# Expert tiles that add their gated results to the output rows, with the addition in the middle of the next tile, and expert weights split over two tiles

## The reference, cut to what matters

```python
N, C, E, H = 4096, 256, 8, 1024
x = x + graph_attention(layernorm(x), adj, Wq, Wk, Wv)     # adj is sparse: a few neighbours a row
xn = layernorm(x)
probs = softmax(xn @ W_router)
topk_p, topk_i = top_k(probs, 2)
topk_p = topk_p / topk_p.sum(-1)
combine = sum of one_hot(topk_i) * topk_p                  # [N, E], two entries a token
for e in range(E):
    h = relu(xn @ W1[e] + b1[e])
    y = h @ W2[e] + b2[e]
    out = out + combine[:, e:e+1] * y
x = x + out
```

## Time and profile before

| | |
|---|---|
| median of 3 runs | 1069.51 us (1068.68 to 1070.36) |
| the profiled execution | 1069.15 us, its span 1067.5 us |
| PE busy | 799.0 us (75%) |
| PEld busy | 731.2 us (68%) |
| DVE busy | 673.1 us (63%) |
| ACT busy | 465.5 us (44%) |
| POOL busy | 440.1 us (41%) |
| mean granted TensorE clock over the span | 0.855 |

### The profile page before, as it was taken

One profiled execution on the slowest core, in us unless ns is written; L12 is line 12 of the kernel. 1 busy time (PEld: TensorE's weight loads), 2 busy tenths in 40 slices (PEclk: granted clock), 3 DMA queues, 4 the chain that ended last, 5 costly groups with the idle time before them and its releaser, 6 DMA issues.

```text
span 1067.5 us, 23696 instructions
## 1 busy us (share of the span) xinstructions
PE 799.0 (75%) x6721; PEld 731.2 (68%) x6722; DVE 673.1 (63%) x1972; ACT 465.5 (44%) x1309; POOL 440.1 (41%) x440
## 2 busy tenths in 40 slices
PE   2559987997799862254606999999999999999900
PEld 1458876886788751253606988889888898889800
DVE  9867877777688653486275465565565646554555
ACT  2333544343355531143303665655555566565600
POOL 5277777777777732167771000000000000007465
PEclk8578999998899985655557999999999999999955
DMA  9741431422321110222356324241423332124345
GB/s 267 242 109 28 105 103 31 108 71 59 81 51 25 28 31 1 72 86 99 138 182 207 118 74 128 81 141 64 138 79 118 100 116 69 59 79 141 105 144 181
DMA packets 108904, 108.32 MB, mean 101 GB/s; under 512 B 18275, under 2 KB 98100, under 8 KB 108720
## 3 DMA queue, kind: packets, MB, share of 16 engines
q1 hardware_dynamic: 85680, 65.32, 20.1%
q0 software_dynamic: 23168, 42.22, 13.4%
HBM read 93.10 MB, written 40.37 MB: 125 GB/s over the span
## 4 chain that ended last, share of the span: by engine, by line
PE 45%; issue 19%; DVE 15%; POOL 13%; DMA 5%; ACT 2%; DVEq 1%; POOLq 1%; SPq 0%; ACTq 0%
PE psE L1179 10%; POOL nbr L439 7%; PE psH L1168 6%; PE psH L1169 6%; PE psH L1170 6%; PE psE L1181 5%; PE psY L1017 4%; POOL expert_in L486 4%; PE codes L980 2%; DMA xg<-expert_out,gpos 2%; DVE prod L593 2%; PE psQ L1027 1%; PE psX L1155 1%; PE psL L1131 1%; DVE best L575 1%
## 5 line engine op out<-in xcount | busy, mean ns | idle before, releaser
L439 POOL DMA_INDIRECT nbr<-xn_rows,idx x256 | 263.1, 1028 | 108.9 <-issue 104.9
L898 DVE TENSOR_TENSOR h_lo<-z_all,h_hi 128x256 fp32r<-128x256 f32 x296 | 125.2, 423 | 156.4 <-ACT h_hi L1354 156.4
L1353 ACT ACTIVATE z_all<-psH,b1e 128x256 f32<-128x256 f32 x296 | 142.0, 480 | 173.4 <-PE psH L1170 173.4
L1179 PE MATMUL psE<-w_parts,h_hi 128*128 128x512 f32 x552 | 210.2, 407 | 1.7 <-DVE h_lo L898 1.4
L1168 PE MATMUL psH<-x_hi,w_hi 128*128 128x256 f32 (+1 forms) x592 | 167.0, 282 | 13.0 <-issue 6.8
L575 DVE MAX8 best<-codes 128x8 f16<-128x1024 f32 x128 | 150.4, 1222 | 36.4 <-PE codes L980 34.0
L1169 PE MATMUL psH<-x_lo,w_hi 128*128 128x256 f32 (+1 forms) x592 | 167.4, 283 | 0.0
L1170 PE MATMUL psH<-x_hi,w_lo 128*128 128x256 f32 (+1 forms) x592 | 167.0, 282 | 0.0
L1181 PE MATMUL psE<-w_parts,h_lo 128*128 128x256 f32 x552 | 155.4, 281 | 0.0
L1354 ACT ACTIVATE h_hi<-psH,b1e 128x256 fp32r<-128x256 f32 x296 | 141.1, 477 | 0.0
L1017 PEld LDWEIGHTS psY<-diag,nbr 128*128 128x128 f32 x1024 | 133.5, 210 | 7.2 <-issue 4.7
(11 more groups left out here) (258 smaller groups left out, 1096.5 us busy)
## 6 DMA issues: line engine op xcount, KB each, us to landing
adj_in<-in_adj SPq DMA_DIRECT2D x8, 2048.0 KB, 11.1
w_raw<-in_L_ffn_W POOLq DMA_DIRECT2D x16, 1024.0 KB, 5.8
x_in<-expert_in SPq DMA_DIRECT2D x38, 256.0 KB, 2.7
expert_out<-y_out SPq DMA_DIRECT2D x37, 256.0 KB
early_out<-y_out SPq DMA_DIRECT2D x32, 256.0 KB, 2.5
nbr<-xn_rows,idx POOLq DMA_INDIRECT x264, 2.2
x_all<-in_x SPq DMA_DIRECT2D x4, 1024.0 KB, 9.2
xn_rows<-row_all SPq DMA_DIRECT2D x4, 1024.0 KB, 5.0
```

The source lines that it names most:

```text
L439: pool.indirect_dma_start(nbr[:, u, k, :], None, xn_rows, bass.IndirectOffsetOnAxis(ap=idx[:, u, k:k + 1], axis=0), bounds_check=N - 1, oo ...
L898: dve.tensor_tensor(h_lo[:, hc, :], h_f[:, hc, :], h_hi[:, hc, :].bitcast(F32), ALU.subtract).then_inc(hl_ready, 1)
L1179: pe.matmul(psE[:, q, :], h_hi[:, hc, m], w2_parts[:, b, hc].rearrange("p s c -> p (s c)"), start=(hc == 0), stop=False)
L1353: act.activation(h_f[:, hc, :], psH[:, hc % 4, 0:T], ACT.Relu, bias=b1e[:, b, hc:hc + 1])
```

## The change

- `expert_in`'s rows get four more columns (`CX` = C + 4): the token's number (`TOK`), its first expert plus E (`FIRST`), and the difference of its two top logits (`LESS`). VectorE writes them into `xg` (`extras_ready`). Rows that only fill a region up carry the token number N, which the bounds check of the indirect DMAs leaves out.
- x2 is stored to the output (`store_x2`), one quarter after another during routing.
- For each tile GpSimd gathers the tokens' present output rows into `acc`, VectorE computes the gate from the extra columns (`gate_of`, four small operations), adds gate x `y_sum` to `acc` (`add_rows`), and GpSimd scatters the result to the output. `add_rows` and `gate_of` stand in front of chunk 4 of the next tile. At the border between two experts the gather waits until the last scatter has landed.
- The two result tables, their positions and gates, the 64 gathers of result rows, the mixing and the last stores go.
- VectorE splits W1's four pieces in an expert's first tile and W2's four in its second, at chunks 1, 3, 5 and 7.
- SyncE, not GpSimd, loads the raw weights.
- VectorE's and ScalarE's programs of the expert stage are written out for each expert, and ScalarE reads `b1T` directly.

```diff
@@ SyncE
+            def load_weights(e, m):
+                if not isinstance(e, int) or e > 0:
+                    wait_alone(sp, w_split, (e - 1) * SPLITS + (m + 1) * (SPLITS // 2))
+                sp.dma_start(matrices[m][1][:], matrices[m][0][bass.ds(e, 1)].rearrange("a (k p) h -> p (a k) h", p=P)).then_inc(w_raw[m], 16)
...
-            load_tile(0, 0)
-
-            with sp.Fori(total, MAX_TILES + 1) as n:
-                sp.dma_start(rows_of(expert_out, n), zero_rows[:].to_broadcast([P, TS, C])).then_inc(rest_zeroed, 16)
...
-            with sp.Fori(1, early + 1) as n:
-                load_tile(n, tile_row(n))
-                store_tile(n - 1, True)
...
+            def tiles(e, weights):
+                count = sp.value_load(plan[0:1, 0, bass.ds(e, 1)], min_val=1, max_val=N // T)
+                before = sp.value_load(plan[0:1, 1, bass.ds(e, 1)], min_val=0, max_val=MAX_TILES)
+                load_tile(before, e * REGION)
+                with sp.If(count > 1):
+                    load_tile(before + 1, e * REGION + T)
+                if weights:
+                    load_weights(e + 2, 0)
+                    load_weights(e + 2, 1)
+                with sp.If(count > 2):
+                    with sp.Fori(2, count) as i:
+                        load_tile(before + i, e * REGION + i * T)
+            with sp.Fori(0, E - 2) as e:
+                tiles(e, True)
+            with sp.Fori(E - 2, E) as e:
+                tiles(e, False)
@@ GpSimd
-            wait_alone(pool, yo_stored, total * 16 + 16)
-            with pool.Fori(0, NG // 2) as g:
-                fetch(g * 2, 0)
-                fetch(g * 2 + 1, 1)
...
+            def rows_of_tile(n, after):
+                wait_alone(pool, marks_ready, n + 2)
+                pool.tensor_copy(tok_next[:], marks[:, :, 0]).then_inc(tok_taken, 1)
+                wait_alone(pool, tok_taken, n + 2)
+                if after:
+                    wait_alone(pool, y_scattered, n * (TS * 16))
+                for q in range(TS):
+                    pool.indirect_dma_start(acc[:, q, :], None, out, bass.IndirectOffsetOnAxis(ap=tok_next[:, q:q + 1], axis=0),
+                                            bounds_check=N - 1, oob_is_err=False).then_inc(acc_ready, 16)
+
+            def add_tile(done):
+                wait_alone(pool, acc_ready, done * (TS * 16))
+                pool.tensor_copy(tok_now[:], tok_next[:]).then_inc(tok_kept, 1)
+                wait_alone(pool, tok_kept, done)
+                for q in range(TS):
+                    wait_alone(pool, y_ready, done * TS + q + 1)
+                    pool.indirect_dma_start(out, bass.IndirectOffsetOnAxis(ap=tok_now[:, q:q + 1], axis=0), y_out[:, q, :], None,
+                                            bounds_check=N - 1, oob_is_err=False).then_inc(y_scattered, 16)
@@ VectorE
+            def add_rows(done):
+                wait_alone(dve, acc_ready, done * (TS * 16))
+                wait_alone(dve, gate_step, done * 4)
+                wait_alone(dve, y_free, done)
+                for q in range(TS):
+                    wait_alone(dve, yo_ready, done * TS + q + 1)
+                    dve.scalar_tensor_tensor(y_out[:, q, :], y_sum[:, q, :], gate[:, 3, q:q + 1], acc[:, q, :],
+                                             ALU.mult, ALU.add).then_inc(y_ready, 1)
...
+            def tile(n, e, split=None, first=False, alone=None):
                 for hc in range(HC):
...
+                    if hc == HC // 2:
+                        if not first:
+                            add_rows(n)
+                        gate_of(n, e)
+                    splitting = split is not None and hc % 2 == 1
+                    c = (split or 0) * (SPLITS // 2) + hc // 2
+                    if splitting:
+                        next_weights_hi(e, c)
                     dve.wait_ge(hf_ready, n * HC + hc + 1 + 4)
                     dve.tensor_tensor(h_lo[:, hc, :], h_f[:, hc, :], h_hi[:, hc, :].bitcast(F32), ALU.subtract).then_inc(hl_ready, 1)
...
+                    if splitting:
+                        next_weights_lo(e, c)
```

More of the change, by code:

```diff
@@ L359, in _ @@
                 sp.sem_inc(xg_free, 1)
+                store_x2(2 + b)
             sp.wait_ge(norm_ready, NT // QT)
@@ L517, in _ @@
+            rows_of_tile(0, False)
+            with pool.Fori(0, E - 1) as e:
+                tiles(e, True)
+            tiles(E - 1, False)
         @block.vector
@@ L902, in tile @@
+                if alone is not None:
+                    with dve.If(alone):
+                        for c in range(SPLITS // 2, SPLITS):
+                            next_weights_hi(e, c)
+                            next_weights_lo(e, c)
                 rest_of_x(n + 1)
-                wait_alone(dve, yo_stored, n * 16 + 16)
                 for q in range(TS):
@@ new lines, in count_of, with before_of @@
+            def count_of(e):
+                return dve.value_load(plan[0:1, 0, e:e + 1], min_val=1, max_val=N // T)
+            def before_of(e):
+                return dve.value_load(plan[0:1, 1, e:e + 1], min_val=e, max_val=MAX_TILES)
+            rest_of_x(0)
+            count, before = count_of(0), 0
+            for e in range(E):
+                last = e + 1 == E
+                tile(before, e, None if last else 0, e == 0, None if last else count < 2)
+                if not last:
+                    next_count, next_before = count_of(e + 1), before_of(e + 1)
@@ L915, in tiles @@
                 with dve.If(count > 1):
-                    with dve.Fori(1, count) as i:
+                    tile(before + 1, e, None if last else 1)
+                with dve.If(count > 2):
+                    with dve.Fori(2, count) as i:
                         tile(before + i, e)
-            rest_of_x(0)
-            with dve.Fori(0, E // 2 - 1) as e:
-                tiles(e * 2, 1)
-                tiles(e * 2 + 1, 0)
-            tiles(E - 2, 1)
-            tiles(E - 1, None)
-            dve.sem_inc(mixed, GT)
@@ L940, in _ @@
-            dve.wait_ge(lower_fetched, 16 * NT)
-            place(0, 0)
-            first = 0
-            for rows in (z_all[:, NT // 2:NT, :], w1_raw[:].rearrange("p k (j c) -> p (k j) c", c=C), w2_raw[:]):
-                groups = rows.shape[1] // GT
-                with dve.Fori(0, groups // 2) as i:
-                    g = i * 2 + first
-                    place(g + 1, 1)
-                    mix(g, 0, lambda u: row(rows, i * (2 * GT) + u))
-                    if first + groups < NG:
-                        place(g + 2, 0)
-                    mix(g + 1, 1, lambda u: row(rows, i * (2 * GT) + (GT + u)))
-                first += groups
+                if not last:
+                    count, before = next_count, next_before
@@ L955, in _ @@
+            add_rows(before + count)
         @block.tensor
@@ L1359, in attention_and_experts @@
+            count, before = count_of(0), 0
+            for e in range(E):
+                tile_of(before, e)
+                if e + 1 < E:
+                    next_count, next_before = count_of(e + 1), before_of(e + 1)
+                with act.If(count > 1):
+                    with act.Fori(1, count) as i:
+                        tile_of(before + i, e)
+                if e + 1 < E:
+                    count, before = next_count, next_before
     return nc
```

272 lines of the change are left out of this document (110 added, 162 removed).

## The result

The changed kernel takes 1085.93 us (median of 3 runs, 1083.92 to 1085.99) against 1069.51 before: a ratio of 1.0147, interval 1.0124 to 1.017. It is slower, by 16 us; the prediction had forecast 12.5. The profiled execution has a span of 1084.1 us and a mean granted clock of 0.847.

A forecast was written before the change was run, and what follows sets the result against it. TensorE, busy 430.5 of the expert stage's 446.4 us, was taken as the bound, with a separate 53.5 us tail. 1067.5 - 48.2 + 1.9 - 5.6 + 64.8 = 1080.4, with 1.65 outside the span 1082 us; 8-in-10 range 1058 to 1098.

The forecast's parts named there:

- Deciding term, SyncE's queue: Expert's third tile load queued behind W2, which awaits the last split: TensorE waits 8.8 us, six times; bounds 6.9 and 11.
- t0: Time of TensorE's transposes after an expert's second tile, when it wants the third tile; last split predicted 2.1 us later.
- The clock: After each of six waits for the third tile, TensorE restarts at 1.2 GHz: 2.0 us each, bounds 0 and 4.
- The rival in which the clock stays up: Third tile's load overlaps or overtakes W2, clock stays up: 6.35 us per expert, 1055 us; chance 0.18.
- The gap that the prediction named as a sign: Between TensorE's transposes: about 22 us in six second tiles, 11.8 elsewhere.
- Splitting in two tiles: VectorE's weight splits spread over an expert's first two tiles: 0.8 us less for each of seven experts, -5.6.
- Start of the stage: Before the first x_in: two SyncE table loads, +1.6 us, and three small VectorE operations, +0.3; together +1.9.
- The 0.3 for the routing: Three small VectorE operations in front of `placed`, before the expert stage: +0.3 us.
- Tail: After the last tile, gathers, additions and output stores go; two additions, two scatters and a landing remain: 48.2 us removed.
- Additions at no cost: add_rows in mid-tile finds its gathered old rows landed: cost 0; if transfers crowd, up to 1 us a tile, 37 us.
- The rival's mechanism: Gathers and scatters land behind 1 MB loads, VectorE stands in add_rows: 1096 us, or 1119 in all tiles; chance 0.22.
- programs written out per expert: Fetching VectorE's and ScalarE's longer programs may show at branches: 0 to 0.5 us for each of 14, taken as 0.

## Why the prediction was right, point by point

- Deciding term, SyncE's queue. Right in place, cause and number of times: six waits, of 8.55 us against 8.8. That the size is so near is partly luck, since inside it two errors cancel: the last split came 1.2 us after t0 and not 2.1, and the tile was used 7.3 after W2's issue and not 6.4. The tile landed 7.0 us after W2's issue (5.9 after its own), where the trace's own start had given 6.3. The Trainium skill, DMA: Bandwidth & Descriptors, section "Anatomy of one DMA", has its fit for DMAs that GpSimd issues; by it 5.0 us for W2 and tile together are an estimate. Here, where SyncE issues both, that is 2.0 us too short. By the Trainium skill, DMA: Bandwidth & Descriptors, section "Queues, rings and completion order", the tile cannot be seen before W2. The trace agrees: W2 lands at 673.2, 6.0 after its issue, and the tile at 674.2. What the order costs is from the runs: with W2 behind the tile, the tile is used 3.2 us sooner.
- The clock: 1.8 us for each wait against 2.0. Kept at work, TensorE pays nothing (11.7 against 13.5). The rival in which the clock stays up was wrong. The gap that the prediction named as a sign, about 22 us between transposes, is 20.4 to 21.2; its own terms give 11.8 + 8.8 = 20.6.
- Splitting in two tiles: right as far as it was asked. The tile after a splitting one took 13.04 in the kernel before; the same tiles now take 12.0 to 12.2 with the wait taken off, and 12.07 in the seventh expert's pass, where there is no wait. That is 0.7 to 0.9 less, once the 0.12 of the tensors' place is taken off. The second tiles give 5.6 us in all, as predicted, though some 0.8 of that is the place; the first tiles give 2.1 more, which the prediction did not count.
- Start of the stage: +5.1 against +1.9. The two table loads are right: from the scatter's landing at 568.03 to the issue at 569.99 are 1.96 us. The 0.3 for the routing is too small. From the first scatter's issue to the last are 84.0 us (481.62 to 565.58), and 83.9 to 84.4 in every experiment on the changed kernel; in the kernel before they are 82.3 (479.84 to 562.17), with the wider `x_in` too. These 1.6 us come with the change, and whether the wider rows make them no run takes apart. The other 1.8 stand at the first scatter already, and need not be the change's: the experiments on the changed kernel alter nothing that stands ahead of the scatters, and their last scatter is issued anywhere from 563.68 to 566.69.
- Tail: -41.5 against -48.2, the term most off. The prediction counted additions, scatters and a landing, and forgot that the last tile has gathers as well: the second is issued at 1073.05, behind `y_sum`, so VectorE waits 2.9 us for it. GpSimd answers VectorE only 0.9 us after the first addition (0.25 was SyncE's), and the end comes 5.6 us after the last scatter's issue, not 2.4; the profile shows no work in the last 4.6 of them. The last matmul is 12.9 us from the end, and not about 6.
- Additions at no cost: right for the changed kernel (two waits, 4.0 us, one of them in the tail). But they were hidden partly by the bad wait itself: where that is gone they cost 1.1 us in each of six tiles. The rival's mechanism is real, its price here 6 us and not 14 to 37. The cost that the prediction took as 0 for programs written out per expert, 0 to 0.5 us at each of 14 places, no run measures by itself.

The sum was 4 us short of the median because start and tail were 10 us too good, and the stage 6 us too dear (59.2 us predicted, 53.0 measured). The deciding mechanism was right; that the total came within 4 us owes something to these errors having opposite signs.

## What to carry to other kernels

When loads move to another engine's queue, read what stands behind each wait in that queue: here one load that had to wait for VectorE stood ahead of one that did not, and moving the second forward by one place turned 1.5% slower into 4% faster. A removed wait uncovers the next one, so count what the long wait was covering (here the late gathers) before summing gains. The additions that must wait for a DMA cost less here in the middle of the next tile than at the border between two tiles, where they delay what TensorE waits for. And before a shift of 2 to 3 us is given to a change, look at how far it moves between runs in which nothing before it differs.

## What the hardware showed that was not expected

- The place of tensors in SBUF changes TensorE's pace: a full tile takes 11.81 us in the kernel before, 11.69 with `x_in` 16 bytes a row wider, some 3 us in all. By which tensor, and why, is open.
- A small gather in GpSimd's queue is held up by a megabyte in SyncE's. Around W2 the two gathers of a pass land 5.6 to 6.2 us after their issue in the changed kernel, around a quarter of W2 3.1 to 3.8. From issue to landing, all 74 gathers of the run with the tile first, then all of the run with a quarter of W2:

```profile
DMA to landing us min/median/max: 2.1/3.4/6.2
...
DMA to landing us min/median/max: 2.1/3.2/4.3
```

- TensorE's clock drops as much after a wait of 5.4 us as after one of 8.6, and is at 2.4 GHz again from 4 us after the restart on; after the restart at 183 us in the kernel before it was still at 1.2 GHz from 4 to 8 us.
- 240 more TensorE instructions in the loop came with stalls of 4.6 and 5.9 us at the start of two experts, both where the loop jumps back; the cause is not shown.
